# Cross-attention with adaptive layer norm: reciprocals in PSUM, a shared bank, a new order of each step, and stores from SyncE

## The reference, cut to what matters

```python
def _ada_ln(x, c, W_ss, b_ss):
    mu = jnp.mean(x, axis=-1, keepdims=True)
    var = jnp.mean((x - mu) ** 2, axis=-1, keepdims=True)
    h = (x - mu) / jnp.sqrt(var + EPS)
    ss = jax.nn.silu(c) @ W_ss + b_ss
    scale, bias = jnp.split(ss, 2, axis=-1)
    return (1.0 + scale)[:, None, :] * h + bias[:, None, :]
# x_q (16, 1024, 512), x_kv (16, 64, 512), t_vec (16, 512), 16 heads of 32
xq = _ada_ln(x_q, t_vec, Wss_q, bss_q)
xkv = _ada_ln(x_kv, t_vec, Wss_kv, bss_kv)
q = (xq @ Wq + bq).reshape(B, Lq, nh, dh)
kv = (xkv @ Wkv + bkv).reshape(B, Lkv, 2, nh, dh)
k, v = kv[:, :, 0], kv[:, :, 1]
scores = jnp.einsum('bqhd,bkhd->bhqk', q, k) / jnp.sqrt(jnp.float32(dh))
attn = jax.nn.softmax(scores, axis=-1)
out = jnp.einsum('bhqk,bkhd->bqhd', attn, v).reshape(B, Lq, H)
return x_q + (out @ Wp + bp)
```

## Time and profile before

| | |
|---|---|
| median of 3 runs | 1285.41 us (1282.66 to 1286.21) |
| the profiled execution's own time | 1281.65 us |
| its span, from the first to the last instruction | 1279.8 us |
| mean granted TensorE clock | 0.979 |
| busy: PE, DVE, POOL, ACT | 1189.2, 1165.7, 972.0, 903.9 us |

### The profile page before, as it was taken

The page is one execution under the profiler, slowest core; times in us unless marked ns, Lnnn a source line. Parts: engine busy times, 40 slices in busy tenths (PEclk is TensorE's granted clock), DMA queues, the critical chain, the costliest instruction groups (busy, mean ns, idle before and its releaser), DMA issues.

```text
span 1279.8 us, 33552 instructions
## 1 busy us (share of the span) xinstructions
PE 1189.2 (93%) x11072; PEld 697.8 (55%) x11072; DVE 1165.7 (91%) x1797; ACT 903.9 (71%) x1688; POOL 972.0 (76%) x1202
## 2 busy tenths in 40 slices
PE   7897899999999999999999999999999999999876
PEld 3674555555555555555555555555555555555443
DVE  5745899999999999999999999999999999999985
ACT  3476677777777777787777777776877768777443
POOL 2543678879797978889797979788797979797544
PEclk9799799999999999999999999999999999999988
DMA  9110232322322223222232322322323223221111
GB/s 334 37 42 25 67 99 76 101 83 89 96 82 93 88 84 98 82 90 93 79 98 82 90 91 81 98 87 85 98 82 90 94 78 98 82 90 66 51 58 58
DMA packets 59865, 111.91 MB, mean 87 GB/s; under 512 B 6412, under 2 KB 6440, under 8 KB 59832
## 3 DMA queue, kind: packets, MB, share of 16 engines
q1 hardware_dynamic: 41400, 77.92, 20.3%
q10 hardware_dynamic: 18432, 33.56, 7.0%
HBM read 77.90 MB, written 33.55 MB: 87 GB/s over the span
## 4 chain that ended last, share of the span: by engine, by line
DVE 54%; issue 23%; PE 8%; ACT 3%; POOL 1%; DVEq 1%; ACTq 1%; POOLq 0%
DVE pr L879 14%; DVE pt_lo L907 10%; DVE pr L899 7%; DVE den L864 5%; DVE mx L887 5%; DVE xT_lo L849 4%; PE ps_q L1136 4%; DVE q_lo L917 3%; DVE oT_lo L856 3%; DVE rden L871 2%; PE ps_t L1170 2%; PE ps_s L1155 2%; DVEq L224 1%; ACT kb L526 1%; ACT xT_hi L509 1%
## 5 line engine op out<-in xcount | busy, mean ns | idle before, releaser
L879 DVE SCALAR_TENSOR_TENSOR pr<-pr,rden 128x512 f32<-128x512 f32 x256 | 295.7, 1194 | 4.4
L425 POOL TENSOR_TENSOR half_den<-pr 128x512 f32<-128x512 f32 x128 | 195.5, 1527 | 106.2 <-ACT pr L619 67.0
L568 ACT ACTIVATE q_hi<-ps_q,cur_bq 128x512 f16<-128x512 f32 x126 | 86.6, 687 | 197.5 <-PE ps_q L1136 173.2
L1170 PE MATMUL ps_t<-ident,pr 128*128 128x128 f32 x1024 | 164.0, 288 | 37.9 <-DVE pr L879 36.0
L418 POOL TENSOR_TENSOR xr<-y,xr 128x512 f32<-128x512 f32 x128 | 178.0, 1391 | 8.9 <-ACT y L534 8.9
L558 ACT CAST pt_hi<-ps_t 128x512 f16<-128x512 f32 x256 | 148.3, 588 | 46.5 <-PE ps_t L1170 41.7
L394 POOL TENSOR_TENSOR xr<-xr,bp_row 128x512 f32<-128x512 f32 x128 | 165.9, 1296 | 13.1 <-POOL rstd L373 6.9
L887 DVE TENSOR_REDUCE mx<-ps_s 128x8 f32<-128x512 f32 x256 | 163.2, 676 | 7.0 <-PE ps_s L1155 6.9
L907 DVE TENSOR_TENSOR pt_lo<-ps_t,pt_hi 128x512 f16<-128x512 f32 x256 | 163.0, 675 | 0.2 <-ACT pt_hi L558 0.2
L899 DVE TENSOR_TENSOR pr<-ps_s,mx 128x512 f32<-128x512 f32 x256 | 162.9, 675 | 0.0
L619 ACT ACTIVATE pr<-pr,exp_scale 128x1024 f32<-128x1024 f32 x128 | 146.2, 1142 | 12.6 <-DVE pr L899 12.2
(11 more groups left out here) (167 smaller groups left out, 2402.5 us busy)
## 6 DMA issues: line engine op xcount, KB each, us to landing
x_in<-in_x_dram SPq DMA_DIRECT2D x128, 256.0 KB, 2.6
xr<-in_x_dram SPq DMA_DIRECT2D x128, 256.0 KB, 2.8
out_dram<-xr ACTq DMA_DIRECT2D x128, 256.0 KB, 2.0
raw<-in_L_xcond_Wss_kv_dram SPq DMA_DIRECT2D x4, 512.0 KB, 5.2
cx<-in_ctx_dram SPq DMA_DIRECT2D x1, 2048.0 KB, 12.1
raw<-in_L_xcond_Wss_q_dram SPq DMA_DIRECT2D x4, 512.0 KB, 12.9
raw<-in_L_xcond_Wkv_dram SPq DMA_DIRECT2D x2, 1024.0 KB, 15.5
wq<-in_L_xcond_Wq_dram SPq DMA_DIRECT2D x1, 1024.0 KB, 16.5
```

The source lines that it names most:

```text
L425: pool.tensor_tensor(half_den[:, :, :], pr[:, off % 2, :, 0:LKV // 2], pr[:, off % 2, :, LKV // 2:LKV], ALU.add).then_inc(half_done, 1)
L879: dve.scalar_tensor_tensor(out=pr[:, off % 2, hs, :], in0=pr[:, off % 2, hs, :], scalar=P_UNIT, in1=rden[:, hs].unsqueeze(2).to_broadcast( ...
L1170: last = pe.transpose(ps_t[:, h, P * g:P * (g + 1)], pr[:, off % 2, 2 * pair:2 * pair + 2, :].rearrange("p h l -> p (h l)"), ident[:, :])
```

## The change

It has several parts, all in one diff:

- `rden`, the reciprocals, is no longer in SBUF but lies in the PSUM bank `ps_v[:, 1]`. The transposed rows move into `ps_v[:, 0]`, which the attention output uses too, so `turn_x` waits for `oT_done`, and `weigh` waits for `xT_done`.
- The order of each engine's step is new. PE: `score(i)`, `turn_p(i-2)` (it was `i-1`, at the end), `project(i+4)`, `turn_x(i+8)`, `project_out(i-3)`, `weigh(i-2)`. The copies of the transposed rows come in the same step (`turned_x(i+8)`, it was `i+7`). The layer norm runs one unit further ahead (`i+9`, it was `i+8`).
- The mean comes straight from ACT's accumulator (scale -1/H); POOL's `mean` is gone. `moments` is two operations instead of three.
- In POOL's step, `scaled_wq_lo` and `scaled_wq` stand ahead of the layer norm and the residual, and in ACT's step `scaled_wq_hi` stands behind `sum_squares(i+9)`, near the end.
- `kb` and `vb` are written by two ACT operations each with a mask of 0 and 1 per partition as scale. `values` moves from step 2 to step 1. POOL's zeroing of the tiles is gone; DVE makes the masks once.
- SP issues the stores, between its loads; a load of the residual rows comes a step later.

```diff
+        rden = ps_v[:, 1, 0:NH]
...
         def x_bank(b, off):
-            return ps_t[:, 0, :] if isinstance(b, int) and unit(b, off) < PER else ps_v[:, 1, :]
+            return ps_t[:, 0, :] if isinstance(b, int) and unit(b, off) < PER else ps_v[:, 0, :]
...
# SyncE
+            def store(b, off):
+                if not exists(b, off):
+                    return
+                wait(sp, y_ready, upto(b, off))
+                sp.dma_start(out_units[unit(b, off)], xr[:, off % 4, :]).then_inc(stored[off % 4], 16)
+
             def step(b, i):
+                store(b, i - 4)
                 load_x(b, i + 12)
-                load_xr(b, i)
+                load_xr(b, i - 1)
...
# GpSimd
-            def mean(b, off):
+            def await_rows(b, off):
 
                 if exists(b, off):
-                    s = off % 2
-                    wait(pool, xh_ready, unit(b, off - 1))
-                    wait(pool, row_stats, 2 * unit(b, off) + 1)
-                    pool.tensor_tensor(neg_mean[:, s:s + 1], row_sum[:, s:s + 1], over_h[:, 0:1], ALU.mult)\
-                        .then_inc(mean_ready, 1)
+                    wait(pool, row_stats, 2 * upto(b, off))
...
-                wait(pool, row_stats, 2 * upto(b, off))
-                pool.tensor_tensor(var[:, s:s + 1], row_sq[:, s:s + 1], over_h[:, 1:2], ALU.mult).then_inc(ln_step, 1)
-                wait(pool, ln_step, 3 * unit(b, off) + 1)
-                pool.tensor_tensor(veps[:, s:s + 1], var[:, s:s + 1], eps[:, :], ALU.add).then_inc(ln_step, 1)
-                wait(pool, ln_step, 3 * unit(b, off) + 2)
+                pool.tensor_scalar(veps[:, s:s + 1], row_sq[:, s:s + 1], 1.0 / H, EPS, ALU.mult, ALU.add)\
+                    .then_inc(ln_step, 1)
+                wait(pool, ln_step, 2 * unit(b, off) + 1)
...
             def step(b, i):
                 half_sums(b, i - 1)
-                mean(b, i + 8)
-                add_rows(b, i - 4)
-                moments(b, i + 8)
-                await_moments(b, i + 8)
-                residual(b, i - 3)
-                normalise(b, i + 8)
                 if 2 <= i <= 5:
                     scaled_wq_lo(b + 1, i - 2)
                 if 1 <= i <= 4:
                     scaled_wq(b + 1, i - 1)
+                await_rows(b, i + 9)
+                residual(b, i - 2)
+                moments(b, i + 9)
+                await_moments(b, i + 9)
+                add_rows(b, i - 4)
+                normalise(b, i + 9)
...
# ScalarE
-                for r in range(HPG):
-                    rows = slice(DH * r, DH * (r + 1))
-                    act.copy(kb[rows, :, :, r % 2, :], k16[rows, b, :, :, :]).then_inc(kb_done, 1)
+                for r in range(2):
+                    act.activation(kb[:, :, :, r, :], k16[:, b, :, :, :], ACT.Copy, scale=k_mask[:, r:r + 1])\
+                       .then_inc(kb_done, 1)
...
-                for part in range(2):
-                    for par in range(2):
-                        rows = slice(LKV * par, LKV * (par + 1))
-                        act.copy(vb[rows, part, :, par, :], v_all[rows, part, b, :, :]).then_inc(vb_done, 1)
+                for par in range(2):
+                    act.activation(vb[:, :, :, par, :], v_all[:, :, b, :, :], ACT.Copy, scale=v_mask[:, par:par + 1])\
+                       .then_inc(vb_done, 1)
...
-                    wait(act, mean_ready, unit(b, off - 1))
-                    act.activation(junk[:, :], x_in[:, off % 4, :], ACT.Copy,
-                                   accum_out=row_sum[:, off % 2:off % 2 + 1]).then_inc(row_stats, 1)
+                    wait(act, xh_ready, unit(b, off - 1))
+                    act.activation(junk[:, :], x_in[:, off % 4, :], ACT.Copy, scale=-1.0 / H,
+                                   accum_out=neg_mean[:, off % 2:off % 2 + 1]).then_inc(row_stats, 1)
...
             def step(b, i):
-                sum_rows(b, i + 8)
                 output(b, i - 4)
-                if not (isinstance(b, int) and b == 0 and i == 0):
-                    turned_x(b, i + 7)
                 turned_o(b, i - 3)
                 turned_p(b, i - 2, 0)
                 turned_p(b, i - 2, 1)
-                sum_squares(b, i + 8)
-                if isinstance(b, int) and b == 0 and i in (0, 1):
-                    wp_high(i)
-                if 2 <= i <= 5:
-                    scaled_wq_hi(b + 1, i - 2)
-                if i == 4:
-                    query_bias(b + 1)
-                if i == 2:
-                    values(b)
-                query(b, i + 4)
-                if i == 7:
-                    key_blocks(b + 1)
+                sum_rows(b, i + 9)
                 if exists(b, i):
...
                     act.activation(pr[:, i % 2], pr[:, i % 2], ACT.Exp, scale=exp_scale[:, 0:1]).then_inc(exp_done, 1)
-                if exists(b, i - 4):
-                    s = (i - 4) % 4
-                    wait(act, y_ready, upto(b, i - 4))
-                    act.dma_start(out_units[unit(b, i - 4)], xr[:, s, :]).then_inc(stored[s], 16)
+                turned_x(b, i + 8)
+                if i == 4:
+                    query_bias(b + 1)
+                query(b, i + 4)
+                sum_squares(b, i + 9)
+                if isinstance(b, int) and b == 0 and i in (0, 1):
+                    wp_high(i)
+                if 2 <= i <= 5:
+                    scaled_wq_hi(b + 1, i - 2)
+                if i == 1:
+                    values(b)
+                if i == 7:
+                    key_blocks(b + 1)
...
# VectorE
             def step(b, i):
-                if not (isinstance(b, int) and b == 0 and i == 0):
-                    turned_x(b, i + 7)
                 turned_o(b, i - 3)
...
                 turned_p(b, i - 2, 1)
+                turned_x(b, i + 8)
                 weight_sums(b, i - 1)
...
# TensorE
                 wait(pe, xT_done, unit(b, off))
...
+                wait(pe, oT_done, upto(b, off - 11))
...
                 wait(pe, oT_done, unit(b, off))
+                wait(pe, xT_done, upto(b, off + 10))
...
             def step(b, i):
                 score(b, i)
+                turn_p(b, i - 2)
                 project(b, i + 4)
+                turn_x(b, i + 8)
                 project_out(b, i - 3)
-                turn_x(b, i + 8)
                 weigh(b, i - 2)
-                turn_p(b, i - 1)
```

More of the change, by code:

```diff
@@ L12 @@
 AX_X = mybir.AxisListType.X
+AX_XY = mybir.AxisListType.XY
 P = 128
@@ L97, in adaln_cross_attention @@
         xr = sb("xr", [P, 4, H], F32)
-        over_h = sb("over_h", [P, 2], F32)
-        var = sb("var", [P, 2], F32)
-        eps = sb("eps", [P, 1], F32)
+        k_mask = sb("k_mask", [P, 2], F32)
+        v_mask = sb("v_mask", [P, 2], F32)
         veps = sb("veps", [P, 2], F32)
@@ L179, in adaln_cross_attention @@
         ld_ssq = [sem(f"ld_ssq{k}") for k in range(KC)]
-        id_zero, id_ready, consts_ready, bd_ready = (
-            sem(n) for n in ("id_zero", "id_ready", "consts_ready", "bd_ready"))
+        id_zero, id_ready, consts_ready, masks_ready = (
+            sem(n) for n in ("id_zero", "id_ready", "consts_ready", "masks_ready"))
         small_turned, c_copied, c_exp, silu_step, mod_mm, mod_copied, mod_turned, mod_ready = (
@@ L202, in adaln_cross_attention @@
         stored = [sem(f"stored{i}") for i in range(4)]
-        row_stats, mean_ready, ln_step, xh_ready, xT_turned, xT_hi_done, xT_done = (
-            sem(n) for n in ("row_stats", "mean_ready", "ln_step", "xh_ready", "xT_turned", "xT_hi_done", "xT_done"))
+        row_stats, ln_step, xh_ready, xT_turned, xT_hi_done, xT_done = (
+            sem(n) for n in ("row_stats", "ln_step", "xh_ready", "xT_turned", "xT_hi_done", "xT_done"))
         sc_staged, w_tmp_done, w_hi_done, w_done = (
@@ L246, in every_step @@
                 step(0, i)
-            with eng.Fori(1, B - 1) as b:
+            with eng.Fori(1, B - 2) as b:
                 for i in range(PER):
                     step(b, i)
-            for i in range(PER):
-                step(B - 1, i)
+            for b in (B - 2, B - 1):
+                for i in range(PER):
+                    step(b, i)
             for i in range(4):
@@ L318, in _ @@
                     step(b, i)
+            for i in range(4):
+                step(B, i)
+            for s in stored:
+                sp.wait_ge(s, 16 * (UNITS // 4))
         @block.gpsimd
@@ L379, in await_moments @@
                     wait(pool, xT_turned, unit(b, off - 1))
-                    wait(pool, ln_step, 3 * upto(b, off))
+                    wait(pool, ln_step, 2 * upto(b, off))
             def normalise(b, off):
@@ L458, in step @@
                     scaled_wq(b + 1, i - 1)
+                await_rows(b, i + 9)
[4 more added lines that the diff above has]
+                normalise(b, i + 9)
             def prime():
                 def layernorm(f):
-                    mean(0, f)
+                    await_rows(0, f)
                     moments(0, f)
```

(16 more changed lines are left out.)

17 lines of the change are left out of this document (4 added, 13 removed).

## The result

The changed kernel takes 1311.55 us (median of 4 runs, 1311.36 to 1312.15), the kernel before 1284.04 beside it (1281.76 to 1286.21). The ratio is 1.0215, with a 95% interval of 1.0194 to 1.0236, so it is clearly slower, by about 2%. The profiled execution took 1311.49 us with a span of 1309.7, against 1279.8 before: +29.9.

The account below looks back on a forecast made before the run. PE and DVE were taken as nearly full, DVE's excess being L879. Fourteen batches +31, the last batch -13.5 and the prologue 0 gave +17.5: 1281.65 to 1299 profiled, median 1303, range 1270 to 1338.

Parts of the forecast that it names:

- Fourteen batches: Batches 1 to 14: each 73.0 us against 70.8, +2.2, together +31.
- the ring: ACT's `w_hi`, POOL's `w_lo` to `xh`, PE's `turn_x`: 9.5 us a turn against 8.31; rival at 45%, 1288 to 1321.
- The last batch: No `turn_x` or next `w` there; DVE gains 2.16 and 1.5 a step, less 1.0 for scores: -13.5.
- L879: DVE's product with the reciprocals: with one PSUM input, 0.65 us a half, bounds 0.65 to 1.73.
- Prologue and batch 0: A layer norm moved ahead, an ACT pass moved behind the exponential: 0, with 4 us either way.
- Scores' wait: PE's scores, now ahead of `turn_p`, wait for DVE's `q_lo`: step 7 to 0 takes 9.3 us.
- Worth nothing by itself: Fewer ACT copies for `kb` and `vb`, and the store's issue off ACT, gain nothing, since ACT had idle time.
- SP's queue: SP's stores stand ahead of two loads used a step or more later: no cost.
- The clock: Rival at 20%: PE's clock falls once a batch, a 7 us stretch costing 2.3 a batch, +32, 1335 us.
- No ring, so faster: Rival at 20%: `w_hi` comes early enough for POOL, a batch takes 69.0 us, the whole kernel 1247 us.
- Same: Rival at 8%: a ring at 9.0 and a hidden `values` wait balance the last batch, 1282 to 1289 us.
- L879 stays slow: Rival at 5%: DVE's product isn't sped up, DVE step 8.85 us, 57 on top, 1360 us.

Follow-up runs that it names:

- e4: The changed kernel with `turn_p` ahead of the scores on PE again, as before the change: 1316.6 us, 1.027 of the kernel before.
- e5: The changed kernel with the reciprocals in SBUF again: 1438.3 us, 1.122 of the kernel before.
- e9: e7 with the reciprocals in SBUF again: 1254.5 us, 0.979 of the kernel before.
- e8: The changed kernel with only `q_lo` moved ahead of sum, reciprocal and product on DVE: 1291.2 us, 1.007 of the kernel before.
- e1: The changed kernel with POOL's `w_lo` and `w_tmp` behind `normalise` again: 1272.8 us, 0.993 of the kernel before.
- e2: The changed kernel with ACT's `w_hi` moved ahead of the row sums in its step: 1246.2 us, 0.972 of the kernel before.
- e6: e2 with `values` in step 2 again, right behind the early `w_hi`: 1232.5 us, 0.961 of the kernel before.
- e12: e7 with the stores issued by ACT at the end of its step: 1575.8 us, 1.229 of the kernel before.
- e7: e6 with `q_lo` moved ahead of sum, reciprocal and product on DVE: 1200.5 us, 0.936 of the kernel before.
- e10: The kernel before with the masks alone, two ACT operations each for `kb` and `vb`, no POOL zeroing: 1260.1 us, 0.983 of the kernel before.

## Why the prediction was right, and where it was off

The forecast was 1303, and the median is 1311.55. The time is right in direction and mechanism and 8.5 too low. That flatters it: its own sum was +17.5 on the profiled execution, and the trace gives +29.9, 12.4 more. The other 3.9 are luck. The forecast added 3.8 because the profiled execution before lay that far below its median, and the one after doesn't (1311.49 and 1311.55). By its terms:

**Fourteen batches: +31 forecast, +47.6 measured** (74.21 on average less 70.81, times 14). This is the mis-sized term. Every engine-to-engine part of the ring is a little longer than put: `w_lo` starts at t + 3.16, not 3.01; from there to the next `turn_x` are 6.62, not 6.49. That is 0.2 to 0.3 in each of the transitions 3→4, 4→5 and 5→6. Step 2→3 is 0.48 over its 11.1: `oT_lo` comes at W + 3.42, not 3.22 (W is 656.06), `xT_hi` at W + 7.59, not 7.4, and the ring's own excess comes on top. Against it the bare steps are 8.20 and 8.26, not 8.31. Small errors in a batch of 73 count fourteen times: 1.2 a batch is 17 us. Some 2 of the 17 come from single batches, 1.0 from the clock (above) and 0.9 from a load (below).

**The last batch: -13.5 forecast, -17.1 measured** (71.9 us from its start to the end against 89.0). By the starts of the scores, the first steps went from 9.5 to 7.8, 1.7 where 1.5 had been put. The last ones went from 9.9 to 6.4, 3.5 where 2.16 had been put for L879. What the sum left out there is the order on PE: before, `turn_p` stood between the product and the scores, and DVE waited for it. e4, which has that order with the fast product, shows the same wait in its last batch; in the kernel before and in e4:

```profile
1243.46 1.29 DVE L887 TENSOR_REDUCE mx<-ps_s 128x8 f32<-128x512 f32 x2 [0.93 <-PE ps_s L1155]
```

```profile
1290.82 1.29 DVE L884 TENSOR_REDUCE mx<-ps_s 128x8 f32<-128x512 f32 x2 [0.93 <-PE ps_s L1152]
```

e4's last two steps on DVE take 7.4, 1.0 over the changed kernel's 6.4. The kernel before also had the lower clock twice for 6.8 us in its last batch, from 1230.2 and from 1250.6, and there the same wait is 2.01; in the changed one it is full from the start of this batch to 1307.2.

**Prologue and batch 0: 0 with 4 either way, -0.6 measured.** The sum of the three is +29.9.

**L879.** Forecast 0.65 a half; the pairs take 1.28 and the mean is 0.684. DVE's gain is on record in e5 and e9: without the PSUM operand the new order would have cost 127 more.

**Scores' wait.** Step 7→0 was 9.38 for a forecast 9.3, and e8 takes out the 1.2 in it. In e1, e2 and e6, where there is no ring to cover it, it comes up in 3→4 too and is larger (1.73 in e6), because `xT_hi` there stands behind an exponential that is itself late.

**"Worth nothing by itself"**, for the masks and the stores, was wrong. The mistake was to read ACT's idle time as an average (96 us of 400): in the step with `kb` it had none in front of `xT_hi`. The sum didn't suffer, since it was built from the new order's own steps. For the stores it was the wait in front of the issue that was overlooked, not the issue: e12. Whether the stores on ACT would have cost as much in the changed kernel, with its rings, was not tried.

**SP's queue** costs next to nothing, as forecast. POOL does wait 72 us in all for residual rows, but nearly always in steps outside the ring:

```profile
L394 POOL TENSOR_TENSOR xr<-xr,bp_row 128x512 f32<-128x512 f32 x128 | 163.0, 1273 | 140.1 <-DMA xr<-in_x_dram 72.1 <-ACT junk L583 68.0
```

One such wait of 2.07 stands at 704.44, and the `turn_x` at 709.44 that follows waits for nothing. The exception is in batch 1: a wait of 0.86 at 251.88 lies in the ring, and step 5→6 takes 9.57 there instead of 8.68.

**The rivals.** The clock did fall inside the batches, which the prediction had named as a sign that it is wrong. But it fell in five of the fourteen and for 3.4 us, not in each for 7, and cost 1.0 us where the rival had 2.3 a batch; over the run it is 0.981, with 0.979 before. So the price was wrong and not only the chance, and e1 and e5 show what the same falls cost without the cover. "No ring, so faster" had 1247, with `w_hi` early as its condition. e2 is that kernel and took 1246.2; two of its terms were off against each other (`values` and the scores' wait larger, the bare step smaller). "Same" doesn't add up: with a ring of 9.0 and the wait of `values` hidden, its batch is 69.9 and the run about 1260; its 1282 to 1289 fit the ring alone, with the wait of `values` left in. Neither came. "L879 stays slow" had a price of 57, and e5 shows 127: 105 in the fourteen batches and the rest at the ends.

**Not tried alone:** the reciprocals in PSUM in the old order, the layer norm one unit further ahead, and the two small POOL operations that went.

## What to carry to other kernels

When a step's order is changed, follow the waits once round from an engine back to itself: four engines that are each busy 69 to 91% can form a ring longer than any of them, and one early wait on the path (`w_hi`, `values`, `q_lo`, a store) is then worth more than a faster operation. An engine's idle share says nothing of one step: a short saving in the one step where it is late is worth its full length. When one of several waits is taken away, expect the next one that it covered, as e2, e6 and e7 did in turn; together they made 1311.6 into 1200.5, though the changed order alone was slower than the old.

## What the runs showed of the hardware

Contention between DVE and POOL slows both: with two SBUF inputs on DVE's side (e5), POOL's `w_lo` grew from 1.162 to 1.416 us on average, and L876 from 0.684 to 1.186. Two masked ACT operations over 128 partitions and 512 columns take 1.32 us (e10), 0.66 each; four copies of `kb` over 32 partitions and 512 columns take 2.53 (before), 0.63 each. The time went by columns, not by partitions. The clock does not follow PE's busy share alone. In e12 PE was busy 300 of 400 us and the clock 1.00 on average, with one fall of 3.4 us (from 851.4); in e5 it was busy 350 of 400 and the clock 0.96:

```profile
600.00:1000.00 400.00, 299.71 (x2872) 171.02 (x2872) 268.40 (x449) 216.76 (x422) 221.04 (x247) 1.00 0.22 68
```

```profile
600.00:1000.00 400.00, 349.79 (x3278) 199.77 (x3278) 338.60 (x508) 254.06 (x474) 272.09 (x279) 0.96 0.23 77
```

What tells the two apart was not tried.
